# Gated cross-attention block: weight transposes through a permuted unit matrix, mask rows by VectorE copies, a new written-out order, the last store in two

## The reference, cut to what matters

```
x = x + tanh(g_x) * attention(layernorm(x), ctx)      # 16 heads of 32, causal mask, softmax
x = x + tanh(g_f) * ffn(layernorm(x))                 # 512 -> 1408 -> 512, silu(gate) * up
# attention: q = x Wq^T; k, v = split(ctx Wkv^T); softmax(mask(q k^T / sqrt(32))) v Wout^T
# ffn: inputs and weights are scaled per row and rounded to fp8 (e4m3), also between up and down
```

## Time and profile before

| | |
|---|---|
| median of 3 runs | 733.21 us |
| profiled execution | 735.42 us, span 733.7 us, granted clock 0.969 |
| PE busy | 664.5 us (91%) |
| DVE busy | 664.1 us (91%) |
| ACT busy | 549.0 us (75%) |
| POOL busy | 546.5 us (74%) |
| DMA packets | 151207, of which 115326 under 512 B |

### The profile page before, as it was taken

The page is one execution under the profiler, slowest core; times in us unless marked ns, Lnnn a source line. Parts: engine busy times, 40 slices in busy tenths (PEclk is TensorE's granted clock), DMA queues, the critical chain, the costliest instruction groups (busy, mean ns, idle before and its releaser), DMA issues.

```text
span 733.7 us, 15607 instructions
## 1 busy us (share of the span) xinstructions
PE 664.5 (91%) x6130; PEld 417.8 (57%) x6130; DVE 664.1 (91%) x1099; ACT 549.0 (75%) x987; POOL 546.5 (74%) x606
## 2 busy tenths in 40 slices
PE   1567889999999999999999999999999999999774
PEld 1456566656666666656565756566666666545331
DVE  5987687999898989999999989999999999899993
ACT  6888768788878796978878787879687868565540
POOL 5777878986868787887878787969597777766551
PEclk9889799999999999999999999999999999999896
DMA  8979875888685749666775757876667664613313
GB/s 308 227 144 201 165 135 99 160 147 158 102 158 92 166 79 195 93 150 110 139 121 136 131 116 143 123 150 112 143 104 147 94 143 76 126 37 78 74 29 96
DMA packets 151207, 95.51 MB, mean 130 GB/s; under 512 B 115326, under 2 KB 121854, under 8 KB 151134
## 3 DMA queue, kind: packets, MB, share of 16 engines
q1 hardware_dynamic: 148974, 92.68, 64.9%
q0 software_dynamic: 576, 1.45, 0.7%
q10 hardware_dynamic: 1584, 0.39, 0.3%
HBM read 31.59 MB, written 9.83 MB: 56 GB/s over the span
## 4 chain that ended last, share of the span: by engine, by line
PE 50%; DVE 24%; ACT 9%; POOL 6%; DMA 5%; issue 2%; SPq 2%; ACTq 0%; POOLq 0%; DVEq 0%
PE pair L1163 30%; PE pair L1401 3%; PE pair L1406 3%; DVE room L2889 3%; PE pair L1432 2%; DVE tm L3240 2%; PE pair L1433 2%; DVE room L3235 2%; POOL PT L799 2%; PE pair L1428 2%; DVE room L2885 2%; DVE mx L3052 2%; DVE room L3278 2%; DVE room L3191 2%; PE pair L1384 1%
## 5 line engine op out<-in xcount | busy, mean ns | idle before, releaser
L835 POOL TENSOR_TENSOR room<-room,up_scale 128x512 f32<-128x512 f32 (+1 forms) x96 | 128.3, 1348 | 38.6 <-ACT room L2303 38.4
L3052 DVE TENSOR_REDUCE mx<-pair 128x6 f32<-128x768 f32 x128 | 116.7, 950 | 4.3 <-PE pair L1339 4.1
L799 POOL TENSOR_SCALAR_AFFINE_SELECT PT<-PT 128x512 f32<-128x512 f32 x128 | 105.6, 854 | 12.4 <-ACT PT L2221 11.7
L2221 ACT ACTIVATE PT<-pair 128x768 f32<-128x768 f32 x128 | 98.0, 816 | 19.3 <-PE pair L1384 16.3
L2303 ACT ACTIVATE room<-room,sx 128x512 f32<-128x512 f32 (+1 forms) x96 | 63.9, 679 | 43.3 <-DVE sx L3156 26.2
L1163 PE MATMUL pair<-WgT,room 128*128 128x512 bf16 (+1 forms) x384 | 91.1, 367 | 4.6 <-DVE room L3235 4.5
L1163 PE MATMUL pair<-WdT,room 128*128 128x512 bf16 x352 | 83.5, 387 | 11.6 <-DMA room<-room 11.6
L1163 PE MATMUL pair<-xT,WqTh 128*128 128x256 bf16 x512 | 88.5, 276 | 4.0 <-ACT x L1979 4.0
L1163 PE MATMUL pair<-WuT,room 128*128 128x512 bf16 (+1 forms) x384 | 91.6, 364 | 0.1
L1163 PE MATMUL pair<-xT,WqTl 128*128 128x256 bf16 x256 | 70.5, 276 | 0.0
L3235 DVE TENSOR_TENSOR room<-pair,room 128x512 f32<-128x512 f32 (+1 forms) x96 | 60.7, 636 | 9.8 <-POOL x L844 6.5
(11 more groups left out here) (137 smaller groups left out, 1854.4 us busy)
## 6 DMA issues: line engine op xcount, KB each, us to landing
xin<-in_x_dram SPq DMA_DIRECT2D x16, 512.0 KB, 4.8
x<-in_x_dram SPq DMA_DIRECT2D x16, 512.0 KB, 3.9
K<-kh SPq DMA_DIRECT2D x32, 256.0 KB, 5.7
Q<-qh SPq DMA_DIRECT2D x32, 256.0 KB, 4.9
out_dram<-x SPq DMA_DIRECT2D x16, 512.0 KB, 3.2
K<-kl SPq DMA_DIRECT2D x16, 256.0 KB, 6.8
Q<-kl SPq DMA_DIRECT2D x16, 256.0 KB, 4.9
room<-in_L_ffn_w_down_dram SPq DMA_DIRECT2D x4, 704.0 KB, 8.0
```

The costliest lines, as they stand in the source:

```text
L799: pool.affine_select(out=view, in_=view, compare_op=ALU.is_ge, fill=0.0, base=0, pattern=[[0, 2], [0, 2], [1, P]], channel_multiplier=-1). ...
L835: pool.tensor_tensor(g, g, up_scale[:, chunk(n)[1]], ALU.mult).then_inc(slw_done, 1)
L2221: act.activation(head_columns(ring(b, c), 0, 384), head_columns(shifted_pair[c][:, :], 0, 384), ACT.Exp, scale=SCALE).then_inc(exp_done, 1)
L3052: dve.tensor_reduce(mx[:, heads, :], head_columns(w, 0, 3 * P).rearrange("p h (r s) -> p h r s", s=P), AX.X, ALU.max).then_inc(max_done, 1)
```

## The change

1. `attention_weights` transposes pieces 0 and 2 to 5 against a permuted view of the unit matrix; the ScalarE copies and the GpSimd subtractions then read and write in order.
2. The mask rows are built at partitions 96 to 124 of two tiles `rows_q` and `rows_k` (with rows of 0 and of -1 at 96 to 98), and four VectorE copies put them into Q4 and K4. Six SP DMAs and `no_maxima(0)` and `no_maxima(1)` are gone.
3. Five of GpSimd's unit roundings (4, 6, 8, 10, 12) are VectorE's.
4. All lists are ordered anew, with later landings of the DMAs counted; a few PSUM banks differ; the loop has the same eight passes with other contents.
5. The last block's output is stored in two halves; VectorE adds the second (`added_last`).

```
-        mask_q = sb("mask_q", [MASK_ROWS, P], BF16)
+        rows_q = sb("rows_q", [P, P], BF16)
...
+            def put_queries(i):
+                dve.tensor_copy(Q4[i][96:MASK_END, :, :].rearrange("r h (t s) -> r (h t) s", t=TT),
+                                rows_q[96:MASK_END, None, :].to_broadcast([MASK_END - 96, NH * TT, P])).then_inc(q_put, 1)
+            def put_keys(i):
+                if i == 0:
+                    dve.wait_ge(const, N_CONST)
...
+            by_place = ident[:, :].rearrange("p (j c) -> p c j", j=G)
-                    last = pe.transpose(bank[aw_bank[n]][:, m * P:(m + 1) * P], src, ident[:, :])
+                    last = pe.transpose(bank[aw_bank[n]][:, m * P:(m + 1) * P], src, ident[:, :] if n == 1 or n >= 6 else by_place)
...
-            if n == 0 or 2 <= n < 6:
-                views = [v.rearrange("p (g c j) -> p g j c", g=KT, j=G) for v in views[:2]] + \
-                    [views[2].rearrange("p (g j c) -> p g j c", g=KT, j=G)]
...
+            def store_half(b, t):
+                if t == 0 and b == 15:
+                    sp.wait_ge(o_added, 31)
+                if t == 1 and b == 15:
+                    sp.wait_ge(o_added_last, 1)
+                sp.dma_start(out[b][tok(t), :], x1[b % NX][:, t, :]).then_inc(stored, 16)
...
+            def added_last(b, t):
+                if b == 15:
+                    dve.wait_ge(y_done, 32)
+                dve.tensor_tensor(x1[b % NX][:, t, :], T[:, t, 0:H], x1[b % NX][:, t, :], ALU.add).then_inc(o_added_last, 1)
```

More of the change, by code:

```diff
@@ L606, in _ @@
+            load_c(15)
+            store(9)
+            no_maxima(14)
+            turn_qx(11, 0)
+            turn_x(14, 0)
+            turn_x(14, 1)
+            load_x1(12)
+            load_x(15)
+            turn_qx(11, 1)
+            stack_keys(14, 0)
+            stack_keys(14, 1)
+            turn_qt(10, 1)
+            stack_keys(14, 2)
+            stack_queries(14, 0)
+            stack_queries(14, 1)
+            store(10)
+            turn_qt(11, 0)
             stack_queries(14, 2)
@@ L1562, in _ @@
             queries(1, 2)
+            queries(1, 3)
+            spread(2)
+            spread(3)
             spread(4)
-            queries(1, 3)
             shifted(0, 0)
@@ L1577, in _ @@
             weighted(0, 3)
-            values(1, 0)
             values(1, 1)
+            unit_turned(9)
+            scores(1, 0)
             unit_turned(11)
-            scores(1, 0)
-            spread(5)
             scores(1, 1)
@@ L1700, in _ @@
-            up_products(1, 3)
-            shifted(3, 4)
-            up_products(1, 4)
-            shifted(3, 5)
-            weighted(3, 0)
-            for k in range(1, 9):
+            for k in range(1, 9):
+                values(k + 2, 0)
+                values(k + 2, 1)
+                down(k - 1, 0)
+                up_products(k, 0)
+                scores(k + 2, 0)
+                gate_products(k, 0)
+                scores(k + 2, 1)
+                scores(k + 2, 2)
+                projected(k + 1, 0)
+                scores(k + 2, 3)
+                projected(k + 1, 1)
+                scores(k + 2, 4)
+                keys(k + 3, 0)
+                scores(k + 2, 5)
+                keys(k + 3, 1)
+                scores(k + 2, 6)
+                gate_products(k, 1)
+                scores(k + 2, 7)
+                gate_products(k, 2)
+                gate_products(k, 3)
+                queries(k + 3, 0)
+                queries(k + 3, 1)
+                turned_maxima(k + 2)
+                up_products(k, 1)
+                gate_products(k, 4)
+                queries(k + 3, 2)
+                gate_products(k, 5)
+                up_products(k, 2)
+                queries(k + 3, 3)
+                projected(k + 1, 2)
+                shifted(k + 2, 0)
+                shifted(k + 2, 1)
+                projected(k + 1, 3)
+                down(k - 1, 1)
+                shifted(k + 2, 2)
+                shifted(k + 2, 3)
+                up_products(k, 3)
+                shifted(k + 2, 4)
+                up_products(k, 4)
+                shifted(k + 2, 5)
+                weighted(k + 2, 0)
@@ new lines, in _ @@
+            values(11, 1)
+            scores(11, 0)
+            up_products(9, 0)
+            gate_products(9, 0)
+            scores(11, 1)
+            scores(11, 2)
+            projected(10, 0)
+            scores(11, 3)
+            projected(10, 1)
+            scores(11, 4)
+            keys(12, 0)
+            scores(11, 5)
+            gate_products(9, 1)
+            scores(11, 6)
+            keys(12, 1)
+            gate_products(9, 2)
+            gate_products(9, 3)
+            scores(11, 7)
@@ new lines, in _ @@
+            up_products(9, 1)
+            queries(12, 0)
+            up_products(9, 2)
+            gate_products(9, 4)
+            turned_maxima(11)
+            queries(12, 1)
+            queries(12, 2)
+            gate_products(9, 5)
+            queries(12, 3)
+            projected(10, 2)
+            projected(10, 3)
+            shifted(11, 0)
+            shifted(11, 1)
+            down(8, 1)
+            shifted(11, 2)
+            shifted(11, 3)
+            up_products(9, 3)
+            shifted(11, 4)
@@ L2331, in abs_t @@
+                if n == 4 and b >= 12:
+                    act.wait_ge(t_done, 6 * b + 5)
+                if n == 5 and 12 <= b <= 14:
+                    act.wait_ge(t_done, 6 * b + 6)
+                if n == 5 and b <= 8:
                     act.wait_ge(t_done, 6 * b + 6)
```

2695 lines of the change are left out of this document (1292 added, 1403 removed).

## The result

The kernel after the change takes 736.63 us (median of 5 runs, 736.04 to 738.38), the kernel before 733.10 (732.18 to 733.24): ratio 1.0052, 95% interval 1.0034 to 1.0070. That is 3.5 us slower, where 2.4 us faster was forecast. The profiled execution took 736.04 us, 1.7 around a span of 734.3.

A forecast was written before the change was run, and what follows sets the result against it. TensorE was taken to bound the middle, VectorE the end, and neither to be full in the start. Start -1.1, middle -0.35, end 0, last store -0.95 gave -2.4: 733.2 to 730.8 us, range 726.5 to 736.5.

The forecast's parts named there:

- The step that failed: Middle: same matmuls in a pass and no idle TensorE time to give; -0.35 us, bounded by -2 and rival 2.
- a little further ahead of the scores that need its bank: Middle: the scaling stands earlier before those scores, so perhaps half of a recorded 0.6 us wait goes.
- Rival 2: Middle: the scores of a pass wait for the maxima; 11 passes by 0.4 us slower, 735.2 us; chance 0.20.
- The start: Up to the sums of block 0: sums 0.5 us earlier, then 0.6 from moving values(1,0); -1.1 us in all.
- That lead is mostly eaten before the sums: Start: first scores 2.5 us earlier, but 8.4 us more VectorE work before the sums, leaving them 0.5 earlier.
- The sign that the prediction gave for being wrong: Start: a granted clock below 0.74 from 80 to 100 us, or a second stretch like it.
- The copies of the mask rows: Start: VectorE copies of 29 x 4096 bfloat16, taken at 1.4 us each, two ahead of the first scores.
- Roundings on DVE: Start: five unit roundings moved to VectorE at 1.21 us each, 6.1 us in all, with 11 us gone from GpSimd.
- Permuted transposes: Start: twenty transposes against the permuted unit matrix cost 0 more, with up to 4 us kept for the range.
- The end: Last add and store: add on VectorE -0.65 us, last store of 256 KB -0.3; together -0.95 us.
- the same steps in nearly the same order; 0: End, from the sums of block 15: VectorE work 50.4 us before, 50.6 after, without the new add; counted 0.
- The shared port: Start: VectorE and GpSimd lock each other out; five fewer GpSimd roundings could give some 3 us more lead; none counted.

The follow-up runs named there:

- The experiment: Kernel after the change with GpSimd's subtraction queries_low(k+3,1) moved behind causal_part(k+2,1) and added(k-1,1), away from lifted_t: 736.25 us, ratio 1.0052.
- the best measured: Kernel after the change with rounded_t behind down_scaled, 733.10 us; kernel before with only the permuted matrix and the new end, 732.71 us; both ratio 0.9994.

## Why the prediction was wrong, by its own steps

- **The step that failed** is *"The list of a pass holds the same matmuls, and PE has no idle time to give"*, with its -0.35 us. Its first half is true. But that TensorE had no idle time to give only bounded the gain; it said nothing of what other loops could take. The loop over DVE, `down_scaled` and TensorE was put at nothing: the pass went from 38.64 to 39.53, and the seven passes from block 2 to block 9 cost 6.3 us. I had noted that the scaled output stands *"a little further ahead of the scores that need its bank"*; measured, second scores wait 0.86 us for it in every pass, where the first scores waited 0.6 us for such a scaling once in 395 us before.
- **Rival 2** had the right sign and kind (DVE's play of 2.2 us used up, TensorE waiting in each pass) and the wrong place: no scores of the middle wait for maxima by more than the 0.3 us of a weight load, the second scores wait for `down_scaled`. Its 735.2 was 1.4 short. It had a chance of 0.20, with the work of DVE counted, and not the collision with GpSimd (0.83 us in one `lifted_t`) nor the rounding moved ahead (1.17).
- **The start** was mis-sized to the other side. First scores at 54.45, forecast 61.5, before 63.99; sums at 89.45, forecast 93.4. *"That lead is mostly eaten before the sums"* was half right: of 9.5 us, 4.5 were left, DVE being busy 19.83 of 20 us from 60 to 80 and again from 80 to 100. Its work between first maxima and sums was counted at 19.2 us before and 27.6 after; the traces have it busy 22.0 and 33.3, so 11.3 us more and not 8.4. The sign that the prediction gave for being wrong, a second stretch with a clock below 0.74, came true (0.69 from 40 to 60), though the start got faster. Some 2 us come from the permuted matrix; the split of the rest among loads and order was not tried.
- **The copies of the mask rows**, 1.4 forecast: 1.22 or 2.07 us, 6.6 in all for the 5.6 counted. The one ahead of the first scores held them:

```profile
52.28 2.07 DVE L2858 COPY Q<-rows_q 29x4096 bf16<-29x4096 bf16 x1
54.45 0.26 PE L1290 MATMUL pair<-K,Q 125*128 125x128 bf16 x1 [2.42 <-DVE Q L2858]
```

- **Roundings on DVE**, 1.21 forecast: 1.55 on average for 128 x 1024. **Permuted transposes**, 0 forecast: 341 ns each, 356 before; right. The groups by shape from 0 to 140 (count, busy us, mean ns, idle before):

```profile
L2851 DVE TENSOR_TENSOR room<-room 128x1024 bf16<-128x1024 f32 x6 | 9.2, 1553 | 0.1
...
L1137 PE MATMUL pair<-ident,PT 128*128 128x128 f32 x32 | 6.3, 341 | 10.9 <-DMA PT<-in_L_xattn_Wq_dram 10.6 <-ACT WdT L1965 0.3
```

- **The end**: the edits brought 1.4 for the 0.95 forecast, the last store of 256 KB landing in 2.0 us; *"the same steps in nearly the same order; 0"* failed by 1.5 us, for which I have no experiment. The traces give a hint: from the sums of block 15 to the end of the last `down_scaled` the same 87 instructions keep DVE busy 53.6 us, before 51.0. Most of what got longer has two inputs in SBUF, as the lift has (roundings of 128 x 1408 from 0.97 to 1.12 us on average, the three lifts of x from 0.74 to 1.00).
- **The shared port**: by the Trainium skill, page "SBUF — State Buffer", section "SBUF: two separate sides", VectorE and GpSimd lock the port pair that they share against each other. The prediction looked for what this rule gives in the start and never asked it about the middle, where a new order sets other instructions beside each other. The experiment agrees with the rule: 2.51 us and 1.68. When the lift started, the subtraction had 1.03 us to go, and the lift lost 0.83; the two don't match exactly, and GpSimd's times are rough.

## What to carry to other kernels

When one engine fills a periodic pass, write down for each wait of the new order the loop that it closes (which step frees the bank, what stands ahead of that step on its engine, who needs the bank), and compare each loop's length with the pass: the longest wins, not the busiest engine, and here idle time outside that loop was worth nothing (1.45 us filled, 0.03 gained). A step moved ahead of the one that frees a bank costs up to its full length as soon as the slack is used, and moving it back gave only the difference to the next loop (39.53 to 38.94, not to 38.64). Look also at what each instruction of DVE with two inputs in SBUF, and each wide copy, will now run beside on GpSimd, and do it again after each move: the rounding that was moved out of one loop met the add.

## What was not expected of the hardware, and what stays open

The same copy of 29 x 4096 bfloat16 took either 1.22 or 2.07 us, nothing between, in all seven profiles that have it. After the change the two of 2.07 ran beside GpSimd's subtractions of 128 x 512, of the two of 1.22 one ran while GpSimd was idle, and one beside a computation on 128 x 2 numbers, which took 1.83 us in place of 0.70. The lift of 128 x 1408 took 1.83 in nearly every pass of the loop before, 2.00 and 2.51 in those after, and 1.67 at its shortest. Small GpSimd instructions suffer as much: in the pass after the change a computation on 128 x 2 numbers, which took 0.19 us before, takes 1.24 beside a lift of DVE (which in turn takes 2.00) and ends at 378.03, within 0.1 us of the lift's end:

```profile
375.98 2.00 DVE L3261 SCALAR_TENSOR_TENSOR room<-room,tmult 128x1408 f16<-128x1408 f32 x1
...
376.79 1.24 POOL L688 TENSOR_SCALAR var_eps<-var 128x2 f32<-128x2 f32 x1 [0.29 <-ACT xcat L2084]
```

Open are three things. The last 0.3 us of the pass with the rounding moved: its chain argues for the loop through `residual(k,1)`, but no kernel with `residual(k,1)` ahead of `lifted_t(k-1,0)`, or with the subtraction at the end of GpSimd's pass, was measured, so that theory 3 (TensorE's order and banks) is excluded for 0.6 of the 0.89 us and not for the rest. The 1.5 us lost in the end. And whether new start, old middle and new end together would beat both kernels: the best measured, at 0.9994 of before twice, don't.
